# Two dense attentions: all scores of a block of keys ahead of all values of the block before it

## The chip, the cores and the metric

The kernel runs on one core of one Trainium2 chip. Its time is the device time of one execution in microseconds (us). Before the change the median of three timed runs is 3114.46 us (3110.84 to 3115.29). The core has five engines with queues of their own, which meet only at semaphores: PE (matmul; its weight loads are listed apart, as PEld), ACT (activation functions), DVE and POOL (element by element), and SP, which here only starts transfers. Each engine works through its queue in the order written.

## The reference

Eight layers on a sequence of 2048 rows of 128 numbers (given as 16 x 128 rows): a windowed attention, a masked feed-forward, a two-way state-space layer, gated experts, a dual attention (dense and sparse), a ternary feed-forward, a plain attention, and an int8 feed-forward. The change touches the dense part of the dual attention and the plain attention. Both are softmax attention with 16 heads of 8 numbers, over all 2048 keys for each sequence as the kernel is given it:

```python
scores = jnp.einsum('bhqd,bhkd->bhqk', q, k) / math.sqrt(dh)
attn = jax.nn.softmax(scores, axis=-1)
ctx = jnp.einsum('bhqk,bhkd->bhqd', attn, v)
```

The plain attention does the same with other scale factors, then projects with `w_o`.

## The kernel before

Layers run one after another. Each layer is made of stages; in a stage every engine has its own list of work, written out by hand in program order, and a barrier stands between stages. No scheduler changes the order.

A dense attention goes in segments and blocks. A segment is a group of four heads and half of the queries (`QC` = 1024 columns); there are 4 x 2 = 8 segments. A segment has `TB` = 16 blocks of 128 keys, numbered on over the segments as `n`, so 128 blocks in all. For a block and each head `j` of the four:

- `head_scores` (line 1550) lets PE compute the scores of 128 keys by 1024 queries into PSUM, as two matmuls of 512 columns (line 1563). The operands `Qs` and `Ks` are bf16 parts of the queries and keys, stacked to 75 rows, so that their product is exact enough; three of the rows carry a guard that keeps the exponentials in range.
- `head_exps` (line 1595) lets ACT take the exponential of the 1024 columns and write it to SBUF (line 1604), in one of `NPT` = 8 buffers `pT`.
- `head_values` (line 1568) lets PE multiply the exponentials with the values (line 1577) and add up over the segment's 16 blocks. It takes one half `c` of the query columns at a time. The four heads' matmuls write to different 32-row strips of PSUM, and run beside each other. In fp32 each goes through PE as two passes, and the trace has a record for each pass.

PSUM holds three score slots of 1024 columns (`NST` = 3) and one accumulator of 1024 columns: it is full. Scores take the slots in turn: turn `4 n + j` uses slot `turn % 3`, and waits until the exponential that read this slot three turns ago is done. ACT waits for the score of its turn. The waits in the code:

```python
    if turn >= NST:                       # line 1556, PE, scores
        pe.wait_ge(expd, turn - NST + 1)
    if c == 0:                            # line 1572, PE, values
        pe.wait_ge(expd, 4 * n + 4)
            act.wait_ge(sps, turn + 1)    # line 1601, ACT
            if j == 0 and turn >= NPT:    # line 1602, ACT
                act.wait_ge(pvd[1], (turn - NPT) // 4 + 1)
```

`expd` counts exponentials done, `sps` scores done, `pvd[c]` value groups done. At the end of a segment DVE copies the accumulator out (line 1667 in the plain attention, 2006 in the dual one); the next segment's first value group of each half waits for that copy.

`head_segments` (line 1583) sets PE's order. It is called once in the plain attention (line 1626, 128 blocks) and twice in the dual attention (line 1970, 64 blocks in each half). In the dual attention DVE and POOL work on the sparse part meanwhile: DVE in `find_cut` and `find_rest`, with the copies of finished segments (`drain`) at set places, and POOL subtracts at line 2028. After each half a stage of its own follows, which begins on PE at line 2069.

Of the kernel before, what the change touches and what calls it, by code (L numbers as in the profile page):

```python
# [7 lines left out]
TB = T // P  # L8
# [1541 lines left out]
def head_scores(pe, g, hd, pT, sps, expd, n, j):  # L1550

    seg, kt = divmod(n, TB)
    hg, qc = divmod(seg, NQ)
    turn = 4 * n + j
    slot = turn % NST
    if turn >= NST:
        pe.wait_ge(expd, turn - NST + 1)
    if kt == 0 and j == 0:
        pe.wait_ge(hd.q_in[qc], hd.QIN * (hg + 1))
        if qc == 0:  # L1560
            pe.wait_ge(hd.k_in[hg % 2], hd.KIN * (hg // 2 + 1))
    for c in range(QC // CH):
        mm = pe.matmul(g.ps[:, slot * QC + c * CH:slot * QC + (c + 1) * CH], hd.Ks[:, hg % 2, j, kt * P:(kt + 1) * P],  # L1563
                       hd.Qs[:, qc, j, c * CH:(c + 1) * CH], start=True, stop=True)
    mm.then_inc(sps, 1)


def head_values(pe, g, hd, pT, expd, accr, pvd, n, c):

    seg, kt = divmod(n, TB)  # L1570
    hg = seg // NQ
    if c == 0:
        pe.wait_ge(expd, 4 * n + 4)
    if kt == 0 and seg:
        pe.wait_ge(accr[c], seg)
    for j in range(4):
        mm = pe.matmul(g.ps[32 * j:32 * j + HS + 1, ACC + c * CH:ACC + (c + 1) * CH],  # L1577
                       hd.Va[:, kt, hg * 4 + j, :], pT[:, (4 * n + j) % NPT, c * CH:(c + 1) * CH],
                       start=(kt == 0), stop=(kt == TB - 1))
    mm.then_inc(pvd[c], 1)  # L1580


def head_segments(pe, g, hd, pT, sps, expd, accr, pvd, first, last):

    for j in range(4):
        head_scores(pe, g, hd, pT, sps, expd, first * TB, j)
    for n in range(first * TB, last * TB):
        for c in range(2):
            if n + 1 < last * TB:
                head_scores(pe, g, hd, pT, sps, expd, n + 1, 2 * c)  # L1590
                head_scores(pe, g, hd, pT, sps, expd, n + 1, 2 * c + 1)
            head_values(pe, g, hd, pT, expd, accr, pvd, n, c)


# [12 lines left out]
def head_attention(nc, g, tag, wqkv, bias, q_scale, k_scale, out_scale, OT):  # L1607


    with ExitStack() as ctx:  # L1610
# [10 lines left out]
        with nc.Block() as block:  # L1621

            @block.tensor
            def _(pe):
                pe.wait_ge(azero, 1)
                head_segments(pe, g, hd, pT, sps, expd, accr, pvd, 0, NSEG)
# [176 lines left out]
def dual_attention(nc, g, I):  # L1803
# [6 lines left out]
    with ExitStack() as ctx:  # L1810
# [5 lines left out]
        with ExitStack() as ctxh:  # L1816
# [59 lines left out]
            for half in range(2):  # L1876
# [77 lines left out]
                with ExitStack() as ctx3:  # L1954
# [11 lines left out]
                    with nc.Block() as block:  # L1966

                        @block.tensor
                        def _(pe):
                            head_segments(pe, g, hd, pT, hps, expd, accr, pvd, first, first + HSEG)  # L1970
# [516 lines left out]
```

## Time and profile before

| | us |
|---|---|
| median of three timed runs | 3114.46 |
| the profiled execution's own time | 3105.74 |
| its span | 3103.7 |
| PE busy | 2384.6 (77%) |
| ACT busy | 1977.1 (64%) |
| DVE busy | 1938.8 (62%) |
| POOL busy | 1068.9 (34%) |
| exponentials of the two dense attentions (L1604) | 495.8 and 496.0 |

The shares are averages over eight different layers. The stretches with the attentions are about 1535 to 1788 us and 1894 to 2148 us (dual), and 2525 to 3027 us (plain). Busy time of PE and PEld overlaps, since weights are loaded while matmuls run; the end of a matmul's record is modelled from its size, its start is not. A row of the timeline merges instructions of one kind that follow each other. In names, `l2m`, `l2x`, `l2s` belong to the dual attention and `l3h`, `l3he` to the plain one; `ps` is PSUM.

### The profile page before, as it was taken

The numbers are of one execution on the slowest core, as the hardware profiler recorded it, in microseconds if no ns is written. First come the engines' busy times: TensorE is split into PE (matmuls) and PEld (weight loads), VectorE is DVE, ScalarE is ACT, GpSimd is POOL, SyncE is SP. The second block draws the span as 40 slices with busy tenths as digits, with TensorE's granted clock in tenths as the row PEclk, the third lists the DMA queues.
The fourth block names the chain that finished last, engine by engine and source line by source line (L and its number), as shares of the span: only waits on it lengthen the run. The fifth ranks groups of instructions, "written<-read, shape, count | busy, mean of one in ns | idle before, by whom it ended". The sixth has DMA issues, their size and how long they took to land. (4 is left out here: it accounts for less than half of the span.)

```text
span 3103.7 us, 32934 instructions
## 1 busy us (share of the span) xinstructions
PE 2384.6 (77%) x12512; PEld 823.1 (27%) x12512; DVE 1938.8 (62%) x2732; ACT 1977.1 (64%) x1894; POOL 1068.9 (34%) x404
## 2 busy tenths in 40 slices
PE   3577777756546676755799988999769859999995
PEld 1122222333112222322222242222434412222223
DVE  5777988758699999887598907986350430121115
ACT  4789999912523333212499947997522249999991
POOL 5889999711079998621000400013000000000000
PEclk8889999979678888887899999999889879999998
DMA  2011121110044544201301020001010030111000
GB/s 72 1 41 41 44 77 43 41 51 8 7 159 156 172 156 153 71 9 54 63 11 26 11 39 1 11 13 43 7 39 0 20 75 14 31 29 26 14 6 27
DMA packets 67032, 144.68 MB, mean 47 GB/s; under 512 B 15607, under 2 KB 30032, under 8 KB 66161
## 3 DMA queue, kind: packets, MB, share of 16 engines
q1 hardware_dynamic: 66864, 142.46, 16.4%
q8 instruction: 103, 1.69, 0.2%
q14 instruction: 65, 0.52, 0.1%
HBM read 117.99 MB, written 24.25 MB: 46 GB/s over the span
## 5 line engine op out<-in xcount | busy, mean ns | idle before, releaser
L601 POOL TENSOR_TENSOR l0a_diff_pool<-l0a_A,l0a_a_of_t 128x2048 f32<-128x2048 f32 x128 | 532.4, 4197 | 34.8 <-ACT l0a_a_of_t L616 34.8
L1604 ACT ACTIVATE l2x_pT<-ps 128x1024 f32<-128x1024 f32 x512 | 495.8, 1021 | 7.3 <-PE ps L1563 5.4
L1604 ACT ACTIVATE l3he_pT<-ps 128x1024 f32<-128x1024 f32 x512 | 496.0, 1021 | 4.1 <-PE ps L1563 2.2
L1069 PE MATMUL ps<-l1s_hc,all_ident 128*128 128x512 f32 x512 | 283.7, 707 | 182.6 <-POOL l1s_hc L1040 100.3
L580 DVE SCALAR_TENSOR_TENSOR l0a_diff_dve<-l0a_A,l0a_pos,ps 128x512 f32<-128x512 f32 x512 | 344.7, 740 | 44.2 <-PE ps L455 44.1
L1031 POOL TENSOR_TENSOR l1s_dBx<-l1a_dtx,l1s_Bs 128x1024 f32<-128x1024 f32 x128 | 297.4, 2353 | 133.3 <-DMA l1s_Bs<-l1a_bc 133.3
L1055 ACT ACTIVATE ps<-l1a_dt,l1a_A 128x1024 f32<-128x1024 f32 x128 | 143.1, 1118 | 274.0 <-DVE l1s_hc L1100 219.9
L1667 DVE COPY l3he_oT<-ps 128x512 f32<-128x512 f32 x16 | 11.1, 691 | 445.2 <-PE ps L1577 445.1
L1563 PE MATMUL ps<-l3h_Qs,l3h_Ks 75*128 75x512 bf16 x1024 | 267.8, 385 | 24.5 <-DVE ps L1652 24.5
L1563 PE MATMUL ps<-l2m_Qs,l2m_Ks 75*128 75x512 bf16 x1024 | 270.2, 388 | 9.8 <-PEq L1886 9.8
L633 ACT ACTIVATE l0a_diff_pool<-l0a_diff_pool 128x2048 f32<-128x2048 f32 x128 | 237.7, 1901 | 53.9 <-POOL l0a_diff_pool L601 53.8
L1577 PE MATMUL ps<-l2x_pT,l2m_Va 128*9 128x512 f32 x2048 | 269.0, 598 | 1.2 <-ACT l2x_pT L1604 1.2
L1577 PE MATMUL ps<-l3he_pT,l3h_Va 128*9 128x512 f32 x2048 | 268.4, 596 | 0.6 <-ACT l3he_pT L1604 0.6
L455 PE MATMUL ps<-l0a_diff_pool,l0a_reducers 128*32 128x512 f32 x1024 | 158.2, 702 | 119.3 <-ACT l0a_diff_pool L633 118.1
L2028 POOL TENSOR_TENSOR l2s_E<-l2s_E,l2x_rest 128x2048 f32<-128x2048 f32 x16 | 72.7, 4545 | 510.6 <-DVEq L1752 505.5
L633 ACT ACTIVATE l0a_diff_dve<-l0a_diff_dve 128x2048 f32<-128x2048 f32 x128 | 237.2, 1897 | 0.3
L1713 DVE TENSOR_SCALAR_CACHE_REDUCE l2x_rest<-l2s_E,l2x_at 128x2048 f32<-128x2048 f32 x96 | 225.2, 2346 | 3.4
L1069 PEld LDWEIGHTS ps<-l1s_hc,all_ident 128*128 128x128 f32 x512 | 109.1, 224 | 357.9 <-POOL l1s_hc L1040 133.4
L455 PE MATMUL ps<-l0a_diff_dve,l0a_reducers 128*32 128x512 f32 x1024 | 150.0, 664 | 50.3 <-ACT l0a_diff_dve L633 48.8
L1563 PEld LDWEIGHTS ps<-l3h_Qs,l3h_Ks 75*128 75x128 bf16 x1024 | 79.8, 98 | 305.3 <-ACT l3he_pT L1604 218.9
L1563 PEld LDWEIGHTS ps<-l2m_Qs,l2m_Ks 75*128 75x128 bf16 x1024 | 80.4, 98 | 292.6 <-ACT l2x_pT L1604 218.3
L1100 DVE TENSOR_TENSOR l1s_hc<-ps,l1s_Cs 128x1024 f32<-128x1024 f32 x86 | 105.3, 1224 | 1.8 <-issue 0.3
(404 smaller groups left out, 3321.8 us busy)
## 6 DMA issues: line engine op xcount, KB each, us to landing
l1s_Bs<-l1a_bc SPq DMA_DIRECT2D x64, 512.0 KB, 3.7
l1s_Cs<-l1a_bc SPq DMA_DIRECT2D x64, 512.0 KB, 4.7
l0a_band_rows<-l0a_band SPq DMA_DIRECT2D x32, 512.0 KB, 5.3
l0a_band<-l0a_exps SPq DMA_DIRECT2D x16, 512.0 KB, 5.1
l2m_Ks<-l2m_parts SPq DMA_DIRECT2D x36, 128.0 KB
l2m_Qs<-l2m_parts SPq DMA_DIRECT2D x72, 64.0 KB
l3h_Ks<-l3h_parts SPq DMA_DIRECT2D x36, 128.0 KB
l3h_Qs<-l3h_parts SPq DMA_DIRECT2D x72, 64.0 KB
```

The source lines that it names most:

```text
L455: mm = pe.matmul(g.ps[32 * c:32 * c + 32, (2 + k) * CH:(3 + k) * CH], wbs[:, k, n, :], ge[:, c, :], start=(n == 0), stop=(n == 3))
L580: ins = dve.scalar_tensor_tensor(out[:, c, :], src[:, c, :], pos[:, d:d + 1], bank(1), ALU.add, ALU.subtract)
L601: pool.tensor_tensor(out, window(s), atb[:, p % 2, :].unsqueeze(1).broadcast_to([P, 4, CH]), ALU.subtract).then_inc(diff_pool, 1)
L633: act.activation(ge, ge, ACT.Gelu).then_inc(gelu_done, 1)
L1031: pool.tensor_tensor(db[:, m % NDB, :], dtx[:, i, h, half * TH:(half + 1) * TH], Bs[:, k % NBS, :], ALU.mult).then_inc(dbd, 1)
L1055: act.activation(hpair(m), dt[:, i, h, half * TH:(half + 1) * TH], ACT.Exp, scale=Al[:, i, h, n:n + 1]).then_inc(dad, 1)
L1069: mm = pe.matmul(g.ps[:, (4 + 2 * h + q) * CH:(5 + 2 * h + q) * CH], g.ident[:, :], hc[:, m % NHC, q * CH:(q + 1) * CH], start=(n == 0), s ...
L1100: dve.tensor_tensor(hc[:, m % NHC, :], hpair(m), Cs[:, k % NCS, :], ALU.mult).then_inc(weighed, 1)
L1563: mm = pe.matmul(g.ps[:, slot * QC + c * CH:slot * QC + (c + 1) * CH], hd.Ks[:, hg % 2, j, kt * P:(kt + 1) * P], hd.Qs[:, qc, j, c * CH:(c ...
L1577: mm = pe.matmul(g.ps[32 * j:32 * j + HS + 1, ACC + c * CH:ACC + (c + 1) * CH], hd.Va[:, kt, hg * 4 + j, :], pT[:, (4 * n + j) % NPT, c * ...
L1604: act.activation(pT[:, turn % NPT, :], g.ps[:, slot * QC:(slot + 1) * QC], ACT.Exp).then_inc(expd, 1)
L1713: step(dve.tensor_scalar(junk[:, b % 2, :], E[:, b, :], at[:, 0, b:b + 1], 0.0, ALU.is_ge, ALU.add, accum_out=at[:, 1, b:b + 1]))
```

## The change

PE's order in `head_segments` changes, and nothing else. Before, the next block's scores come in two pairs, each followed by one half of this block's values. Now all four scores of the next block come first, and both halves of this block's values follow.

```diff
     for n in range(first * TB, last * TB):
+        if n + 1 < last * TB:
+            for j in range(4):
+                head_scores(pe, g, hd, pT, sps, expd, n + 1, j)
         for c in range(2):
-            if n + 1 < last * TB:
-                head_scores(pe, g, hd, pT, sps, expd, n + 1, 2 * c)
-                head_scores(pe, g, hd, pT, sps, expd, n + 1, 2 * c + 1)
             head_values(pe, g, hd, pT, expd, accr, pvd, n, c)
```

The first place is on PE around the scores of the plain attention's third block, as it stands before: the last value group of the first block, two scores, and the first value group of the second block. `9x512` is a value matmul, `128x512` a score matmul (two to a score). The program reuses semaphores, and the name in brackets is the one that a semaphore had in its first use: `l0a_o_done` stands here for `expd`.

```order
L1577 MATMUL ps<-l3he_pT,l3h_Va 9x512 x4
L1563 MATMUL ps<-l3h_Qs,l3h_Ks 128x512 [waits l0a_o_done]
L1563 MATMUL ps<-l3h_Qs,l3h_Ks 128x512
L1563 MATMUL ps<-l3h_Qs,l3h_Ks 128x512 [waits l0a_o_done]
L1563 MATMUL ps<-l3h_Qs,l3h_Ks 128x512
L1577 MATMUL ps<-l3he_pT,l3h_Va 9x512 [waits l0a_o_done]
L1577 MATMUL ps<-l3he_pT,l3h_Va 9x512 x3
```

The same place on PE after the change:

```order
L1577 MATMUL ps<-l3he_pT,l3h_Va 9x512 x7
L1563 MATMUL ps<-l3h_Qs,l3h_Ks 128x512 [waits l0a_o_done]
L1563 MATMUL ps<-l3h_Qs,l3h_Ks 128x512
L1563 MATMUL ps<-l3h_Qs,l3h_Ks 128x512 [waits l0a_o_done]
L1563 MATMUL ps<-l3h_Qs,l3h_Ks 128x512
L1563 MATMUL ps<-l3h_Qs,l3h_Ks 128x512 [waits l0a_o_done]
L1563 MATMUL ps<-l3h_Qs,l3h_Ks 128x512
L1563 MATMUL ps<-l3h_Qs,l3h_Ks 128x512 [waits l0a_o_done]
L1563 MATMUL ps<-l3h_Qs,l3h_Ks 128x512
L1577 MATMUL ps<-l3he_pT,l3h_Va 9x512 [waits l0a_o_done]
L1577 MATMUL ps<-l3he_pT,l3h_Va 9x512 x7
```

The third and fourth score of a block moved up past the first value group, and the two value groups now stand together as eight matmuls. The second place is the start of the plain attention on PE, before; the three semaphores of its first row are the ones of the loads and of the cleared accumulator.

```order
L1563 MATMUL ps<-l3h_Qs,l3h_Ks 128x512 [waits ln4_norm_ready,ln4_ht_ready,l0a_tanh_done]
L1563 MATMUL ps<-l3h_Qs,l3h_Ks 128x512 x5
L1563 MATMUL ps<-l3h_Qs,l3h_Ks 128x512 [waits l0a_o_done]
L1563 MATMUL ps<-l3h_Qs,l3h_Ks 128x512
L1563 MATMUL ps<-l3h_Qs,l3h_Ks 128x512 [waits l0a_o_done]
L1563 MATMUL ps<-l3h_Qs,l3h_Ks 128x512
L1563 MATMUL ps<-l3h_Qs,l3h_Ks 128x512 [waits l0a_o_done]
L1563 MATMUL ps<-l3h_Qs,l3h_Ks 128x512
L1577 MATMUL ps<-l3he_pT,l3h_Va 9x512 [waits l0a_o_done]
L1577 MATMUL ps<-l3he_pT,l3h_Va 9x512 x3
```

Here six scores stand ahead of the first value group, the first three of them without a wait on an exponential. After the change eight do, and the first two value groups follow them. The lists of ACT, DVE, POOL and SP are the same before and after.

## Rows read from the trace of the kernel before

**Rows 1.** Page, costliest groups: xcount, busy us, mean ns, idle before, releaser.

```profile
L1604 ACT ACTIVATE l3he_pT<-ps 128x1024 f32<-128x1024 f32 x512 | 496.0, 1021 | 4.1 <-PE ps L1563 2.2
L1563 PE MATMUL ps<-l3h_Qs,l3h_Ks 75*128 75x512 bf16 x1024 | 267.8, 385 | 24.5 <-DVE ps L1652 24.5
L1577 PE MATMUL ps<-l3he_pT,l3h_Va 128*9 128x512 f32 x2048 | 268.4, 596 | 0.6 <-ACT l3he_pT L1604 0.6
```

**Rows 2.** Busy time by stretch: us, busy (instructions) by engine, PEclk, DMA share, GB/s.

```profile
1600.00:1700.00 100.00, 100.00 (x621) 21.92 (x614) 90.95 (x144) 99.61 (x104) 0.00 (x0) 1.00 0.17 28
2600.00:2700.00 100.00, 100.00 (x622) 21.97 (x615) 9.04 (x4) 99.61 (x104) 0.00 (x0) 1.00 0.15 26
```

**Rows 3.** Waits from 2600 to 3000: total us, times, longest us.

```profile
PEld ps L1563 <- ACT l3he_pT L1604: 176.7, 206, 0.9
```

**Rows 4.** Timeline, weight loads, from 2801.8: start us, us, [idle before <-releaser].

```profile
2801.89 0.12 PEld L1577 LDWEIGHTS ps<-l3he_pT,l3h_Va 128*9 128x9 f32 x8 [0.42 <-issue]
2802.87 0.55 PEld L1563 LDWEIGHTS ps<-l3h_Qs,l3h_Ks 75*128 75x128 bf16 x4 [0.86 <-ACT l3he_pT L1604]
2803.84 0.12 PEld L1577 LDWEIGHTS ps<-l3he_pT,l3h_Va 128*9 128x9 f32 x8 [0.42 <-ACT l3he_pT L1604]
```

**Rows 5.** Timeline, ACT, the same stretch, in short windows of one exponential each.

```profile
2801.57 1.02 ACT L1604 ACTIVATE l3he_pT<-ps 128x1024 f32<-128x1024 f32 x1
2802.49 1.02 ACT L1604 ACTIVATE l3he_pT<-ps 128x1024 f32<-128x1024 f32 x1
2803.51 1.02 ACT L1604 ACTIVATE l3he_pT<-ps 128x1024 f32<-128x1024 f32 x1
...
2805.46 1.02 ACT L1604 ACTIVATE l3he_pT<-ps 128x1024 f32<-128x1024 f32 x1
```

**Rows 6.** Timeline, PE, the same stretch, in short windows of one matmul each.

```profile
2802.32 0.61 PE L1577 MATMUL ps<-l3he_pT,l3h_Va 128*9 128x512 f32 x4
2802.87 0.39 PE L1563 MATMUL ps<-l3h_Qs,l3h_Ks 75*128 75x512 bf16 x1
2803.10 0.38 PE L1563 MATMUL ps<-l3h_Qs,l3h_Ks 75*128 75x512 bf16 x1
2803.31 0.38 PE L1563 MATMUL ps<-l3h_Qs,l3h_Ks 75*128 75x512 bf16 x1
2803.53 0.38 PE L1563 MATMUL ps<-l3h_Qs,l3h_Ks 75*128 75x512 bf16 x1
```

**Rows 7.** Timeline, the plain attention's start: second score matmul, first exponential, fourth score's load.

```profile
2525.60 0.63 PE L1563 MATMUL ps<-l3h_Qs,l3h_Ks 75*128 75x512 bf16 x1
2526.27 1.02 ACT L1604 ACTIVATE l3he_pT<-ps 128x1024 f32<-128x1024 f32 x1 [1.05 <-PE ps L1563]
...
2527.35 0.11 PEld L1563 LDWEIGHTS ps<-l3h_Qs,l3h_Ks 75*128 75x128 bf16 x1 [0.31 <-ACT l3he_pT L1604]
```

**Rows 8.** Timeline, the plain attention's end: last exponential, then both last value groups.

```profile
3024.31 1.02 ACT L1604 ACTIVATE l3he_pT<-ps 128x1024 f32<-128x1024 f32 x1
3025.38 0.12 PEld L1577 LDWEIGHTS ps<-l3he_pT,l3h_Va 128*9 128x9 f32 x8 [1.55 <-ACT l3he_pT L1604]
...
3026.68 0.61 PE L1577 MATMUL ps<-l3he_pT,l3h_Va 128*9 128x512 f32 x4
```

**Rows 9.** Timeline, end of the dual attention's first half, POOL, PE and DVE.

```profile
1780.80 4.54 POOL L2028 TENSOR_TENSOR l2s_E<-l2s_E,l2x_rest 128x2048 f32<-128x2048 f32 x1 [2.55 <-DVEq L1759]
1786.21 1.91 PE L1577 MATMUL ps<-l2x_pT,l2m_Va 128*9 128x512 f32 x16 [0.62 <-ACT l2x_pT L1604]
1787.40 1.48 DVE L2006 COPY l2s_oT<-ps 128x512 f32<-128x512 f32 x2 [6.73 <-PE ps L1577]
```

**Rows 10.** A stretch after the first half; then PE's first scores and values (plain attention).

```profile
1818.00:1858.00 40.00, 33.71 (x131) 17.01 (x130) 3.38 (x14) 23.13 (x32) 2.69 (x2) 0.96 0.01 1
...
2525.20 5.30 PE L1563 MATMUL ps<-l3h_Qs,l3h_Ks 75*128 75x512 bf16 x12 [24.54 <-DVE ps L1652]
2530.43 1.90 PE L1577 MATMUL ps<-l3he_pT,l3h_Va 128*9 128x512 f32 x8
```

## The prediction, made before the changed kernel ran

> **What bounds the kernel now.** I read the page's groups first, then the busy time by stretch, then the waits, and last the timeline of a single block of keys. The groups [rows 1] show the plain attention's 512 exps (L1604), its scores (L1563) and values (L1577); the reader is to see that an exp takes 1.02 us and that 512 of them fill 496 us of one attention. By stretch [rows 2] ACT is busy 99.61 of 100 us in both attentions, PE 100 of 100, and the granted clock is 1.00, which is the 2.4 GHz level. The waits [rows 3] say that the weight load of a score stood idle 206 times "until ACT", 0.9 us each. Taken alone this looks like an ACT-bound loop with PE waiting in it. The timeline says otherwise.
>
> ACT's starts [rows 5] alternate: 2801.57, 2802.49 (0.92 later), 2803.51 (1.02 later), and 2805.46, two exps further. An exp lasts 1.02 but the next can start 0.92 after it; it does so every second time. Where it is late, look at PE [rows 6]: the second matmul of a score starts at 2803.10 and ends at 2803.48, and the exp starts at 2803.51. The same distance stands at the attention's start [rows 7], at half the PE clock: score done at 2525.60 + 0.63 = 2526.23, exp at 2526.27. So ACT waits 0.10 us for a score in every pair, hidden in its busy time because the exp before lasts just as long; its own pace would be 4 x 0.92 = 3.68 us for a block, and the block takes 2805.46 - 2801.57 = 3.89.
>
> PE makes a half block in 1.95 us [rows 4]: values at 2801.89, scores at 2802.87, values at 2803.84. From [rows 6]: last value pass to first score matmul 2802.32 to 2802.87, 0.55; score matmuls 0.23, then about 0.215 twice (2803.10, 2803.31, 2803.53); last score to values 0.31 (to 2803.84). The two value passes (fp32 goes as two passes over four heads at once) stand 0.43 apart. 0.43 + 0.55 + 0.23 + 0.43 + 0.31 = 1.95: nothing is left in which PE could wait. In [rows 4] one value group is put down to ACT and the next to "issue", with the same 0.42 of idle weight port; only the first has a semaphore to wait for. So these "waits" are other matmuls running. The costs beyond streaming are the two kinds of switch: 0.55 against 0.43 (0.12) and 0.31 against 0.215 (0.095). PE, in its order of work, sets the pace.
>
> **The change, part by part.** 256 blocks run (64 in each half of the dual attention, 128 in the plain one). In 63 + 63 + 127 = 253 of them a next block follows, and only there does the order differ. No instruction is added or removed; ACT, DVE, SP and POOL keep theirs.
>
> *What goes.* Two of four switches in a block: 0.12 + 0.095 = 0.215 us of PE. That value groups can follow each other without a switch is seen at the end of the attention [rows 8]: passes from 3025.38 to 3026.68, three steps of 0.43. PE alone would then need 1.30 + 0.55 + 0.23 + 6 x 0.215 + 0.31 = 3.68 us, which equals ACT's own 3.68.
>
> *What is now late.* Line 1557 makes score turn t wait for exp t - 3, since there are three slots. The fourth score of a block (j = 3) so waits for the first exp of the same block, and that exp needs the first score. Before, a value group stood between: the exp is done and seen 0.61 + 0.035 + 1.02 + 0.055 = 1.72 us after the first score starts, and the fourth score's turn came at 1.95 + 0.23 + 0.215 = 2.39, 0.67 to spare. Now its turn comes at 0.23 + 5 x 0.215 = 1.31, and it stands for 0.41 us. Behind it in PE's queue are both value groups, and behind these the next block's first score, for which ACT waits. Nothing can pass.
>
> *The price.* The closed chain, once around: from the first of a block's four value passes to the last 1.30 [rows 8]; last pass to first score 0.55 [rows 6]; that score until done 0.61 (2802.87 to 2803.48); to the exp's start 0.035 [rows 5, 6, 7]; exp 1.02; exp's end to weight load 0.055, from 2526.27 + 1.02 to 2527.35 and from 3024.31 + 1.02 to 3025.38 [rows 7, 8]; fourth score to values 0.23 + 0.31 = 0.54 [rows 6]. Sum 4.11; with rounding of the starts I take 4.10. The other waits have room: the nearest is the third score's, on the previous block's last exp, with about 0.5 us. Against 3.89 that is +0.21 a block, and 253 x 0.21 = +53 us.
>
> *What the rows don't show.* (a) Value groups with no switch in mid-stream: 0 extra by [rows 8], at most the 0.12 of the score switch; I take 0, the row being of the same instructions. (b) The step from exp to weight load when PE is idle but warm: 0.05 to 0.06 in both rows, I take 0.055; 0.10 would add 11 us in all. (c) The first blocks run at half clock, two or so in each walk; there PE alone is the bound and two switches fewer gain, so these three starts are worth within ±1 us. Bounds of the period: 4.07 to 4.23, so +46 to +86.
>
> *Who else hears of it.* In the first half of the dual attention POOL's last subtraction ends at 1780.80 + 4.54 = 1785.34, PE at 1788.12, and DVE stood 6.73 us for PE before its last drain [rows 9]. DVE's drain of the third segment would come about 48 x 0.21 = 10 us later and move POOL's end to 1795, still before PE's 1788 + 13 = 1801. So nothing hides the 13 us of a half. Drains have more room than before, not less, and the next segment's loads are asked for by exp counts a segment ahead.
>
> Against this reading stands a rule of the Trainium skill (TensorE: Matmul & The Clock Gate, The mechanism): a weight load overlaps running matmuls only if its row group differs. All value loads use the same 128 rows, so by the rule each value group would wait for its load, the 0.12 of (a), and the sum would be +84. The trace disagrees at [rows 8], where the passes keep 0.43.
>
> **The rivals.** *PE's saving wins (faster).* If the fourth score's wait were met in time, block and ACT would both run at 3.68: 253 x -0.21 = -53, 3061 us. For it: the saved switches are real, and ACT's scores start in a row. It decides by whether first score to seen exp (1.72) is under the fourth score's turn (1.31); it is not, by 0.41, and no one duration there can be off by that. Chance 0.06.
>
> *No change.* If ACT's 1.02 were its own pace, as its 99.61% suggests, PE would only shuffle work inside ACT's time: 3114. Against it: [rows 5] show 0.92, and the chain of 4.10 is longer than 3.89 whichever is the bound now. Chance 0.04.
>
> *Value groups or the seen exp cost more (slower still).* The 0.12 of (a): period 4.22, +84, 3198. Chance 0.07.
>
> *The clock falls.* PE stands 0.41 us in each block, near 10%. The stretch after the first half [rows 10] shows PE busy 33.71 of 40 us at 0.96 granted, so less dense work held the upper level nearly throughout. At 1.2 GHz scores start 5.30 / 12, some 0.43 us apart, and a value group costs 0.85 more ([rows 10] against the 1.05 us of a warm one by its last pass), so PE needs about 7 us a block: +790, 3900. The skill has a case for it (the same page, A second HAM failure mode: psum-queue depth-cycling): short idle times between groups while PSUM slots cycle made the clock swing. No steady block in this trace does. Chance 0.03.
>
> **How the numbers follow.** Forecast, 0.80: +53 on the profiled execution's own 3105.74 (span 3103.7) gives 3159. That execution lies 8.7 below the median of the timed runs, 3114.46; the times to be compared are timed ones, so 3167. Its own range is 3157 to 3180 (period within 0.03, and the 2 us by which runs differ). Rivals: 0.06, 0.04, 0.07, 0.03. The range 3153 to 3192 takes in the middle of (a) and leaves out under 0.2. A difference under 0.2% (6 us) can't be told from none: faster 0.06, same 0.04, slower 0.90.
>
> **What would show it.** ACT's starts in steady state: 0.92, 0.92, 0.92, 1.34. PE: eight score matmuls, the seventh 0.41 us late on their cadence (0.25 us of nothing between the records, its weight load 0.05 after an exp's end), then sixteen value records in 1.90 us. ACT idle 0.3 us before every fourth exp, put down to PE, and ACT near 92% in [rows 2]'s stretches. Clock still 1.00. The exps of the plain attention span about 525 us instead of 498. I am wrong if exps stand 0.92 apart throughout (the first rival), if the fourth score never waits, or if the hole sits elsewhere.

## The result and the profile after

The changed kernel takes 3164.43 us (median of four runs, 3161.42 to 3165.2), beside 3114.88 for the kernel before on the same chip. The ratio is 1.0147, 95% interval 1.0126 to 1.0168: slower by about 50 us. The forecast was 3167. The profiled execution took 3164.44 us (span 3162.3).

The page's costliest groups first, against [rows 1]: the exps now have 43.1 us of idle time before them instead of 4.1, and of the scores' idle time 31.8 us is put down to ACT. The busy time of the exps fell by 13 us, since more of them start while the one before still runs.

```profile
L1604 ACT ACTIVATE l3he_pT<-ps 128x1024 f32<-128x1024 f32 x512 | 482.7, 1030 | 43.1 <-PE ps L1563 43.1
L1563 PE MATMUL ps<-l3h_Qs,l3h_Ks 75*128 75x512 bf16 x1024 | 268.4, 386 | 61.6 <-ACT l3he_pT L1604 31.8
L1577 PE MATMUL ps<-l3he_pT,l3h_Va 128*9 128x512 f32 x2048 | 244.7, 595 | 0.3 <-ACT l3he_pT L1604 0.3
```

The stretches of [rows 2] (columns as there): ACT from 99.61 to 92.28 of 100 us, in the dual and in the plain attention alike, PE to under 94, the granted clock still 1.00.

```profile
1600.00:1700.00 100.00, 93.69 (x588) 23.34 (x590) 83.72 (x132) 92.28 (x99) 0.00 (x0) 1.00 0.17 28
2700.00:2800.00 100.00, 93.80 (x590) 23.42 (x594) 11.86 (x6) 92.28 (x99) 0.00 (x0) 1.00 0.14 25
```

The waits from 2600 to 3000 us (total us, times, longest us), against [rows 3]. The last two lines are new; the weight loads' line, which was mostly other matmuls running, is much as it was.

```profile
PEld ps L1563 <- ACT l3he_pT L1604: 156.9, 196, 0.9
...
ACT l3he_pT L1604 <- PE ps L1563: 31.5, 98, 0.3
PE ps L1563 <- ACT l3he_pT L1604: 24.7, 98, 0.3
```

One block on PE's timeline, against [rows 4, 6]. Six score matmuls run in their cadence, then PE stands 0.25 us before the fourth score's two, then all sixteen value records follow at once.

```profile
2862.16 1.47 PE L1563 MATMUL ps<-l3h_Qs,l3h_Ks 75*128 75x512 bf16 x6
2863.88 0.61 PE L1563 MATMUL ps<-l3h_Qs,l3h_Ks 75*128 75x512 bf16 x2 [0.25 <-ACT l3he_pT L1604]
2864.42 1.91 PE L1577 MATMUL ps<-l3he_pT,l3h_Va 128*9 128x512 f32 x16
2866.26 0.39 PE L1563 MATMUL ps<-l3h_Qs,l3h_Ks 75*128 75x512 bf16 x1
```

ACT in the same block, against [rows 5]:

```profile
2862.81 1.02 ACT L1604 ACTIVATE l3he_pT<-ps 128x1024 f32<-128x1024 f32 x1 [0.32 <-PE ps L1563]
2863.73 1.02 ACT L1604 ACTIVATE l3he_pT<-ps 128x1024 f32<-128x1024 f32 x1
2864.63 1.03 ACT L1604 ACTIVATE l3he_pT<-ps 128x1024 f32<-128x1024 f32 x1
2865.53 1.04 ACT L1604 ACTIVATE l3he_pT<-ps 128x1024 f32<-128x1024 f32 x1
2866.90 1.02 ACT L1604 ACTIVATE l3he_pT<-ps 128x1024 f32<-128x1024 f32 x1 [0.32 <-PE ps L1563]
```

The starts are 0.92, 0.90, 0.90 and 1.37 apart, a block of 4.09 us where before had 3.89. The chain can be read off both fences. The first score starts at 2862.16 and its exp at 2862.81 (0.65). The exp ends at 2863.83, and the fourth score starts at 2863.88 (0.05). The values follow 0.54 later, and the next first score 1.84 after them. 0.65 + 1.02 + 0.05 + 0.54 + 1.84 = 4.10, the 4.09 of the exps with rounding.

### The profile page after: what moved, and what is told of

It reads as the page before. It is cut to its first block and busy times, and to the rows that moved or that the text cites. A ratio compares the mean times of both kernels' runs of the same rounds, so it can differ in the third digit from the quotient of the medians.

```text
span 3162.3 us, 32934 instructions
## 1 busy us (share of the span) xinstructions
PE 2377.2 (75%) x12512; PEld 851.5 (27%) x12512; DVE 1938.6 (61%) x2732; ACT 1950.6 (62%) x1894; POOL 1069.0 (34%) x404
## 5 line engine op out<-in xcount | busy, mean ns | idle before, releaser
L1604 ACT ACTIVATE l2x_pT<-ps 128x1024 f32<-128x1024 f32 x512 | 482.6, 1031 | 47.6 <-PE ps L1563 47.6
L1604 ACT ACTIVATE l3he_pT<-ps 128x1024 f32<-128x1024 f32 x512 | 482.7, 1030 | 43.1 <-PE ps L1563 43.1
L1563 PE MATMUL ps<-l3h_Qs,l3h_Ks 75*128 75x512 bf16 x1024 | 268.4, 386 | 61.6 <-ACT l3he_pT L1604 31.8
L1577 PE MATMUL ps<-l2x_pT,l2m_Va 128*9 128x512 f32 x2048 | 247.0, 600 | 0.6 <-ACT l2x_pT L1604 0.6
L1577 PE MATMUL ps<-l3he_pT,l3h_Va 128*9 128x512 f32 x2048 | 244.7, 595 | 0.3 <-ACT l3he_pT L1604 0.3
```

What stands on the lines that cost most here:

```text
L1604: act.activation(pT[:, turn % NPT, :], g.ps[:, slot * QC:(slot + 1) * QC], ACT.Exp).then_inc(expd, 1)
```

## The experiments

All eleven kernels of this section change the dense attentions of the dual and the plain layer, if nothing else is said. "Block" is the distance of a block's first exp to the next block's, in the middle of the plain attention.

**Is it the run of four scores?** The first kernel puts three scores in a row, with as many switches as before.

```diff
-                head_scores(..., n + 1, 2 * c)
-                head_scores(..., n + 1, 2 * c + 1)
+                for j in ((0, 1, 2), (3,))[c]:
+                    head_scores(..., n + 1, j)
```

> Order of a block: three scores, values of the first half, the fourth score, values of the second half. Same four switches as before, but three scores in a row instead of two. My theory (a run of four scores closes a chain through the first exp): with three in a row no score needs an exp of its own run; the fourth score's turn comes at 0.23 + 2 x 0.215 + 0.31 + 0.43 + 0.55 = 1.95 us, after the exp is seen at 1.72. PE stays the bound with four switches: period 3.89 us, time as before, 3115. ACT's late exp is now one in four (0.91, 0.91, 0.91, 1.16). Rival (every score moved ahead of the values delays them and with them the loop, in proportion): period about half way, 4.0, and +25 us.

Measured: 3113.01 us, ratio to before 0.9989 (0.9975 to 1.0003), block 3.89, exps 0.92, 0.90, 0.90, 1.16 apart. Moving a score forward costs nothing by itself. The expectation left out two matmuls of the three scores: the fourth score's turn comes 2.38 us after the block's first score (2703.54 to 2705.92), not 1.95, so it has more room than was written. PE without a stall, three scores and one:

```profile
2703.54 1.47 PE L1563 MATMUL ps<-l3h_Qs,l3h_Ks 75*128 75x512 bf16 x6
2704.94 1.05 PE L1577 MATMUL ps<-l3he_pT,l3h_Va 128*9 128x512 f32 x8
2705.92 0.61 PE L1563 MATMUL ps<-l3h_Qs,l3h_Ks 75*128 75x512 bf16 x2
2706.46 1.04 PE L1577 MATMUL ps<-l3he_pT,l3h_Va 128*9 128x512 f32 x8
```

**Is it that the values are queued behind the wait?** The second kernel puts both value groups ahead of the fourth score.

```diff
+        for j in range(3 if more else 0):
+            head_scores(..., n + 1, j)
         for c in range(2):
             head_values(..., n, c)
+        if more:
+            head_scores(..., n + 1, 3)
```

> Order of a block: three scores, both value groups, the fourth score. Two switches as in the changed kernel, but the fourth score stands behind the values, next to the following block's three. My theory: four scores still stand in a row (the fourth and the next three), the last of them waits for the exp of the first of them, the chain has the same members: period 4.10 us, +50 us, the stall moved to the third score of a block. Rival (the harm is that the value groups are queued behind the fourth score's wait): no value is behind it now, the two saved switches win, period 3.68 and -50 us.

Measured: 3163.72 us, ratio 1.0145 (1.0114 to 1.0176), block 4.09. The four scores in a row are now a fourth and the next block's first three, and the same 0.25 stands before the last of them:

```profile
2699.80 1.47 PE L1563 MATMUL ps<-l3h_Qs,l3h_Ks 75*128 75x512 bf16 x6
2701.52 0.61 PE L1563 MATMUL ps<-l3h_Qs,l3h_Ks 75*128 75x512 bf16 x2 [0.25 <-ACT l3he_pT L1606]
2702.06 1.91 PE L1577 MATMUL ps<-l3he_pT,l3h_Va 128*9 128x512 f32 x16
```

Which score comes first does not matter, only how many stand in a row against three slots.

**Who was the bound before, and does a shorter exp turn the sign?** Two kernels with exps of half the columns, in either order.

```diff
-  hd.Va[...], pT[..., c * CH:(c + 1) * CH],      # in head_values
+  hd.Va[...], pT[..., 0:CH],
...
-  act.activation(pT[:, turn % NPT, :], g.ps[:, slot * QC:(slot + 1) * QC], ACT.Exp)
+  act.activation(pT[:, turn % NPT, 0:CH], g.ps[:, slot * QC:slot * QC + CH], ACT.Exp)
```

> The order of before; each exponential covers only the first 512 of a score's 1024 columns, and both value halves read these (the other half of the exponentials is left out). The exp then takes about 0.6 us, an estimate between nothing and 1.02. My theory (PE is the bound before): period unchanged, 3.89 us, time about 3110. Rival (ACT at 99.6% busy is the bound): the period falls, at least 0.2 a block, to where PE's streaming ends, and the time by 50 us or more.

> The changed order with the same halved exponentials (the other half left out). My theory: the chain loses about 0.43 and falls to PE's own need with two switches, 3.68 us a block; against the run with halved exponentials in the old order that is -0.21 a block, about -53 us: the sign of the change turns. Rival (long PE runs cost for a reason of PE's own, such as weight loads or PSUM): it stays 0.2 a block slower than the old order.

Measured, one run each: 3114.02 us and block 3.89 in the old order, 3060.20 and block 3.67 in the changed one. The sign of the change turned: -54 us, by single runs; by the block, which a trace shows many times over, -0.22 us. In the old order ACT is busy 55.65 of 100 us and the kernel has not moved, so ACT was not the bound before, though its row in [rows 2] reads 99.61. The stretch from 2700 to 2800 of the old order, then ACT in it, then PE in the changed one:

```profile
2700.00:2800.00 100.00, 100.00 (x622) 21.97 (x615) 18.18 (x8) 55.65 (x103) 0.00 (x0) 1.00 0.14 29
```

```profile
2701.15 1.08 ACT L1604 ACTIVATE l3he_pT<-ps 128x512 f32<-128x512 f32 x2 [0.86 <-PE ps L1563]
```

```profile
2700.70 1.90 PE L1563 MATMUL ps<-l3h_Qs,l3h_Ks 75*128 75x512 bf16 x8
2702.53 1.90 PE L1577 MATMUL ps<-l3he_pT,l3h_Va 128*9 128x512 f32 x16
2704.37 1.90 PE L1563 MATMUL ps<-l3h_Qs,l3h_Ks 75*128 75x512 bf16 x8
```

Eight score matmuls go without a hole, and 2704.37 - 2700.70 = 3.67 is PE's own need with two switches.

**ACT's own pace, and the change where PE has room.** Two kernels with a light second value group, in either order.

```diff
+        wd = 64 if c else CH
-        mm = pe.matmul(g.ps[..., ACC + c * CH:ACC + (c + 1) * CH], ...)
+        mm = pe.matmul(g.ps[..., ACC + c * CH:ACC + c * CH + wd], ...)
```

The matmul reads only the same `wd` columns of `pT`, and in the plain attention the accumulator is set to 1.0 at the start instead of 0.0.

> The order of before; the second value group of a block has 64 columns instead of 512 (the other 448 columns of the second half's values are left out). PE needs about 0.75 less a block, 3.15. My theory: PE is no longer the bound, ACT runs at its own pace, four times 0.90 to 0.92, 3.65 us a block: -0.24 x 253 = -60 us. Rival (ACT's pace is the 0.97 of before): 3.89, no change.

> The changed order with the same light second value group (448 of its columns left out). My theory: the chain through the first exp loses the same 0.75 and needs 3.35, under ACT's own pace: 3.65 as with the old order, the change costs nothing here. Rival (a run of four scores costs ACT or PE something outside that chain): it stays slower than the old order by about 0.2 a block.

Measured, one run each: 3063.79 and 3055.02 us; block 3.67 in both. The expected 3.65 was missed by 0.02, and the reason is in the ends of the exps, not in their starts. In the changed order with the light group:

```profile
2689.82 1.35 ACT L1605 ACTIVATE l3he_pT<-ps 128x1024 f32<-128x1024 f32 x1
2690.73 1.37 ACT L1605 ACTIVATE l3he_pT<-ps 128x1024 f32<-128x1024 f32 x1
2691.67 1.34 ACT L1605 ACTIVATE l3he_pT<-ps 128x1024 f32<-128x1024 f32 x1
```

The starts are 0.91 and 0.94 apart, but the ends (2691.17, 2692.10, 2693.01) about 0.92; over several blocks they stand 0.917 apart in both kernels, whatever the starts do, and 4 x 0.917 = 3.67. That is ACT's own pace. Where starts run ahead of the ends, the record is longer: 1.02 us in the kernel before, 1.07 to 1.10 in the old order here, 1.34 to 1.37 in the changed one. With ACT as the bound the change costs nothing per block, though the fourth score still waits 0.31 us for ACT.

The 9 us between the two runs do not come from the blocks' pace. Some 6 of them lie behind block 48 of the dual attention's halves, where PE starts the fourth segment and needs DVE's copy of the third. DVE makes this copy at a fixed place in its own list; in the kernel before, PE never waited for it. Both kernels here come to it early. The changed order waits 1.16 us (first row). The old order waits 2.11 us in the first half, and there the granted clock falls to its lower level for 6.8 us (second row), which makes the two blocks from there on 6.08 and 5.47 us long.

```profile
1721.27 1.16 PE L1578 MATMUL ps<-l2x_pT,l2m_Va 128*9 128x512 f32 x16 [1.16 <-DVE l2s_oT L2007]
```

```profile
1722.90:1729.80 6.90, 6.90 (x28) 1.42 (x26) 6.79 (x5) 4.22 (x5) 2.47 (x1) 0.51 0.14 23
```

So a block of about 3.7 us meets a second bound in the dual attention. The changed order with halved exps shows it too: one block there takes 5.12 us instead of 3.67.

**Slots.** The old order with two score slots; the accumulator stays where it is.

```diff
-NPT, NST = 8, 3
-ACC = NST * QC
+NPT, NST = 8, 2
+ACC = 3 * QC
```

> The order of before with two score slots instead of three: score t now waits for exp t - 2. My theory (a score's wait reaches back as many turns as there are slots, and the chain sets the loop when the run reaches that far): the fourth score needs the second exp, seen 0.645 + 0.91 + 1.02 + 0.055 = 2.63 us after the block's first score starts, against a turn of 2.39; it waits 0.25 and the two scores after it find theirs in time: period 4.15, +65 us. Rival (slots play no part in the old order, PE only streams): 3.89.

Measured, one run: 3187.88 us, +71 against the median before; block 4.15, the fourth score late (a pair of scores takes 1.29 us in place of 1.04 in every second group) and 0.27 of idle time before every fourth exp:

```profile
2701.30 3.88 ACT L1604 ACTIVATE l3he_pT<-ps 128x1024 f32<-128x1024 f32 x4 [0.27 <-PE ps L1563]
2705.44 2.97 ACT L1604 ACTIVATE l3he_pT<-ps 128x1024 f32<-128x1024 f32 x3 [0.27 <-PE ps L1563]
```

A chain of the same kind with other members, through the second exp, and the block comes out to the hundredth. The time is less good a witness: of the 71 us some 10 lie at the start of the dual attention's first half, where the clock stayed at its lower level for 31.6 us after the first score; in the trace of before it was 7.8 us.

**One attention alone.** The changed order in the plain attention, the old one in the dual.

> The changed order in the plain attention alone, 127 of the 253 blocks with a next one. My theory: the price is per block and all exposed: 127 x 0.205 = +26 us, half of the change, and the dual attention's halves stay at 249 us between first and last exp. Rival (part of the dual attention's loss hides behind DVE and POOL): more than half of the change's +50, up to all of it, sits here.

Measured: 3137.19 us, ratio 1.0083 (1.0056 to 1.0110), +17 to +34 by the interval. In its trace ACT is busy 99.60 of 100 us from 1600 to 1700 and 92.28 from 2700 to 2800; the halves of the dual attention stay at 3.89 a block. Between first and last exp they take 249.3 and 251.4 us, where the changed order takes 262.9 and 262.3. So the plain attention has about half of the price, and the dual one does not hide its own; the interval alone would also allow the plain one a third or two thirds.

**Shortening the chain.** If the wait for the first exp is the whole price, only that exp needs to be shorter. It is computed in two halves, and the fourth score's matmuls each wait for their half. Nothing is left out.

```diff
-    if turn >= NST:
-        pe.wait_ge(expd, turn - NST + 1)
+    if turn >= NST and j < 3:
+        pe.wait_ge(expd, exps_before(turn - NST + 1))
     for c in range(QC // CH):
+        if j == 3:
+            pe.wait_ge(expd, 5 * n + 1 + c)
...
-    mm.then_inc(sps, 1)
+        if j == 0 or c == 1:
+            mm.then_inc(sps, 1)
...
+            for c in range(2 if j == 0 else 1):
+                cols = slice(c * CH, (c + 1) * CH) if j == 0 else slice(0, QC)
+                act.wait_ge(sps, exps_before(turn) + c + 1)
+                act.activation(pT[:, turn % NPT, cols], ..., ACT.Exp).then_inc(expd, 1)
```

`exps_before` counts five exps to a block, and the other counts of exps follow it.

> The changed order, and the first exponential of each block goes as two of 512 columns: the first starts when the first score matmul is done, and each of the fourth score's two matmuls waits only for the half that it overwrites. All is computed. From the halved runs a 512-column exp takes 0.60 us and the next starts 0.48 to 0.49 later. My theory (the chain through the first exp is the whole price): first score matmul to first half exp 0.43, second half 0.49 later, done and seen 0.65 later = 1.57 against a turn of 1.52; around the chain 1.57 + 2.15 = 3.73 us a block, ACT's own pace is now about 3.70. So 0.16 a block under before, 253 x 0.16 = -41 us against before, about -90 against the changed kernel. Rival (the stall has another cause than that exp's length): 4.10 or more, since ACT has one instruction more in each block.

> The order of before with the same split of the first exponential; the control to the run before it. My theory: PE is the bound and no score waits for an exp, so the split changes nothing: period 3.89, time as before. Rival (the split itself gives the gain, by giving ACT its input earlier or freeing slots earlier): some 0.1 to 0.2 a block under before here too.

Measured: the changed order with the split takes 3085.60 us, ratio to before 0.9903 (0.9884 to 0.9921); the old order with it 3122.65, ratio 1.0014 (0.9999 to 1.0028), block 3.89. So the split alone gives nothing, the order alone loses, and both together gain. The size was missed, -30 where -41 was expected, since the block is 3.785 and not 3.73. The score matmul ends at 2700.51 + 0.39 = 2700.90 and its half exp starts at 2701.00:

```profile
2700.51 0.39 PE L1570 MATMUL ps<-l3h_Qs,l3h_Ks 75*128 75x512 bf16 x1
...
2701.00 0.60 ACT L1614 ACTIVATE l3he_pT<-ps 128x512 f32<-128x512 f32 x1
```

I had written ACT's wait for the values ahead of its wait for the score. The last kernel changes these two lines about.

```diff
-            if j == 0 and turn >= NPT:
-                act.wait_ge(pvd[1], ...)
             ...
                 act.wait_ge(sps, exps_before(turn) + c + 1)
+                if j == 0 and c == 0 and turn >= NPT:
+                    act.wait_ge(pvd[1], ...)
```

> As the run with the split first exponential in the changed order, but ACT's two waits before a block's first half exp change places: the wait for the score is named first and the one for the values two blocks back second, as the original has it. That run's period was 3.785 instead of 3.73: its first half exp started 0.10 us after the score matmul's end and not 0.035, with a semaphore instruction of ACT between (2700.94) and the exp (2701.00). My theory: the instruction that carries the second wait now stands on the values, which are long done, and the exp starts 0.035 after the matmul: period 3.73, another -0.055 x 253 = -14 us. Rival (ACT itself is saturated at 3.78 with five exps a block): no change.

Measured: 3071.20 us, ratio to before 0.9858 (0.9836 to 0.9880), block 3.73: another -14 us against the run before it, by the two ratios, as expected. It beats both kernels: 1.4% under before, 2.8% under the changed one by the two ratios. On PE there is no hole between the records; the eight score records take 1.96 us, and 1.90 with halved exps, because the last matmul of the fourth score still comes 0.05 late. ACT is shown from a block's second half exp to the next block's first:

```profile
2700.08 1.96 PE L1570 MATMUL ps<-l3h_Qs,l3h_Ks 75*128 75x512 bf16 x8
2701.97 1.90 PE L1585 MATMUL ps<-l3he_pT,l3h_Va 128*9 128x512 f32 x16
2703.81 1.96 PE L1570 MATMUL ps<-l3h_Qs,l3h_Ks 75*128 75x512 bf16 x8
```

```profile
2701.00 0.60 ACT L1614 ACTIVATE l3he_pT<-ps 128x512 f32<-128x512 f32 x1
2701.48 1.04 ACT L1614 ACTIVATE l3he_pT<-ps 128x1024 f32<-128x1024 f32 x1
2702.38 1.05 ACT L1614 ACTIVATE l3he_pT<-ps 128x1024 f32<-128x1024 f32 x1
2703.29 1.06 ACT L1614 ACTIVATE l3he_pT<-ps 128x1024 f32<-128x1024 f32 x1
2704.24 0.60 ACT L1614 ACTIVATE l3he_pT<-ps 128x512 f32<-128x512 f32 x1
```

The ends of these exps stand 0.92 apart (0.49 for a half exp) all the way round, and 3 x 0.917 + 2 x 0.49 = 3.73. So ACT is now at its own pace as well. The rival of a saturated ACT had the right engine and a limit 0.05 too high, and by these ends a still shorter chain would gain nothing here (not tried). DVE's third copy costs this kernel 0.1 and 0.4 us in the two halves.

## Why the prediction was right

**The bound before.** PE, not ACT, as the starts of [rows 5] said against the busy share of [rows 2]. Halving the exps moved nothing; lightening PE moved the block to 3.67. ACT's own pace, forecast at 3.68, was 3.67.

**The saved switches.** Forecast 3.68 us of PE a block with two switches; 3.67 measured where the chain is out of the way. The value groups follow each other without a switch in mid-stream too: sixteen records in 1.91, as at the attention's end [rows 8], so term (a) was 0. The rule of the Trainium skill that a weight load overlaps running matmuls only if its row group differs (TensorE: Matmul & The Clock Gate, The mechanism) would have cost 0.12 us a block, and the trace disagrees with it here as it did there.

**The closed chain.** Forecast 4.10, measured 4.09. Its members: score to exp 0.65, exp 1.02, exp to load 0.05, fourth score to values 0.54, values to first score 1.84, against 0.645, 1.02, 0.055, 0.54 and 1.85. The experiments bear it out from four sides: the run's length (three in place of four: gone), its place (shifted: same), the exp's length (halved: gone; split: 3.73, where ACT's own pace is reached too) and the number of slots (two: 4.15).

**The sum.** Between first and last exp the halves of the dual attention grew from 249.2 and 248.8 us to 262.9 and 262.3, the plain attention from 498.0 to 523.6: 52.7 together, against 53. Of this 253 blocks at 0.2015 are 51.0, and the three starts are some 2. The timed medians differ by 49.6 (39 to 52 by the interval), so +53 was a little high.

Term (c), that the three starts are worth "within ±1" because two switches fewer gain there, did not hold: they cost more, and no gain is seen. The second block took 6.81, 6.18 and 5.62 us where it took 5.32, 4.91 and 5.08. Ahead of the third block's first score PE has the same work in both orders; what differs is the clock. The stretch from the first half's first score to the third block's, before and after:

```profile
1534.88:1544.24 9.36, 9.36 (x33) 2.09 (x33) 9.36 (x16) 6.91 (x8) 0.00 (x0) 0.58 0.53 88
```

```profile
1534.71:1545.17 10.46, 10.46 (x33) 2.46 (x33) 10.36 (x26) 7.44 (x8) 0.00 (x0) 0.50 0.52 88
```

The granted clock rose 7.8, 6.9 and 7.4 us after the first score before, and 11.3, 9.9 and 8.8 us after it now. In that first half it rose after 7.8 to 8.0 us in all five traces with the old order and three slots, and after 11.3 to 14.6 us in all five with the changed order. So the later rise goes with the order; why is open. That the sum came out at 52.7 beside 53 is partly luck: the starts were some 2 us too low in it, and 0.20 a block against 0.21 took 2 us back.

**Who else hears of it.** In the first half of the dual attention POOL ended at 1795.7 (forecast 1795) and PE at 1801.6 (1801), against [rows 9]; DVE waited 9.88 us for PE. PE still ends the half, and nothing covers its 13 us.

```profile
1791.17 4.55 POOL L2028 TENSOR_TENSOR l2s_E<-l2s_E,l2x_rest 128x2048 f32<-128x2048 f32 x1 [2.55 <-DVEq L1759]
1799.72 1.90 PE L1577 MATMUL ps<-l2x_pT,l2m_Va 128*9 128x512 f32 x16 [0.31 <-ACT l2x_pT L1604]
1800.91 1.48 DVE L2006 COPY l2s_oT<-ps 128x512 f32<-128x512 f32 x2 [9.88 <-PE ps L1577]
```

**From span to time.** The spans of the two profiled executions differ by 58.6, not by 52.7. Five of the rest lie between the attentions, in a wait for three small stores ahead of the plain attention's loads (the first row of each fence is a store's issue, the second what waits for all three). Before:

```profile
2509.38 1.24 SPq L1362 DMA_DIRECT2D l3h_mparts<-l3hg_guard_parts  x3
2515.18 3.02 SPq L1315 DMA_DIRECT2D l3h_Qs<-l3h_parts  x9
```

After:

```profile
2536.66 1.24 SPq L1362 DMA_DIRECT2D l3h_mparts<-l3hg_guard_parts  x3
2547.45 3.02 SPq L1315 DMA_DIRECT2D l3h_Qs<-l3h_parts  x9
```

That is 5.80 and 10.79 us. From the last store's issue to the next load it is 5.0 to 10.9 us over the thirteen traces of this case, whatever the kernel, and 5.0 is the one of before. So the 8.7 us by which that profiled execution lay under its median can in part be this wait. The forecast added its 53 us to the median, 3167, and not to the profile, 3159; the measured 3164.43 lies between the two, and the spread of the runs does not decide between them. The "2 us by which runs differ" was too small: runs of before ranged over 3107.89 to 3124.23, and their medians from 3111.86 to 3119.13. And a period within 0.03 and these 2 us give 3177 as the upper end of the forecast's own range, not 3180.

**The rivals.** "No change" fell with the halved exps. "PE's saving wins" comes true where the chain is cut: -0.22 a block against the old order with halved exps, where -0.21 was the price. "Value groups or the seen exp cost more" fell with the sixteen records in 1.91 us and the 0.05 from exp to score. "The clock falls" did not happen with the change: 1.00 in all steady stretches, with a hole of 0.25 us in every 4.09. It did happen in another kernel, the old order with the light group, behind a hole of 2.11 us.

**What the prediction did not look at.** "Drains have more room than before, not less" is true of a longer block. Of a shorter one it is not: the forecast's faster rival would have met DVE's third copy, as the kernels with a block of 3.67 did.

## What to carry to other kernels

With k buffers between two engines in a ring, a run of k + 1 producer steps contains a step that waits for the consumer of the run's own first step; that closed the chain here. Keep runs to at most k, or shorten what the first consumer step takes. Runs of at most k are not enough by themselves: with two slots the runs of two still cost 0.26 us a block (4.15). Before ordering work for fewer switches, add up the chain through the step k turns back, and compare it with the period. And judge a pipelined engine by the distance of its ends, not by its busy share. Here an exp's record is longer than the distance at which exps can follow each other, so a wait of up to the difference, 0.10 us, does not show as idle time. When a loop gets faster, look for work of a third engine at a fixed place beside it, such as a copy of the accumulator: it does not get faster with it.

## What the runs showed of the hardware

- Exps of 1024 fp32 columns from PSUM end 0.917 us apart where ACT is the bound, exps of 512 columns 0.49 one behind the other. Their records are longer, 1.02 and 0.60 us, and the next starts 0.90 to 0.92 and 0.48 to 0.49 after. In the changed order with the light value group the records grew to 1.37 us at the same distance of the ends.
- The order of two waits on one ACT instruction is worth 0.06 us. When the wait that ends last is the second one in the program, the exp starts later: 0.10 from matmul end to exp instead of 0.035, and 3.785 against 3.73 a block.
- PE can stay at the lower of its two clock levels for long though it is never idle. In the old order with the split, the second half of the dual attention ran at 0.50 from its start at 1895 until past 1920, with 7.29 us a block (two halves of 3.65), and took 260.2 us from first to last exp where the kernel before had 248.8 and the one with only the plain attention changed 251.4. The forecast had put such a block at about 7. The old order with two slots shows the same in the first half: 0.50 until 31.6 us after its first score. Why the clock rose so late in these two executions is open.

```profile
1900.00:1907.00 7.00, 7.00 (x24) 1.00 (x18) 6.61 (x25) 4.21 (x6) 0.00 (x0) 0.50 0.00 0
1914.00:1950.00 36.00, 36.00 (x192) 7.14 (x191) 34.78 (x49) 30.27 (x39) 0.00 (x0) 0.84 0.00 1
```
